# Cross-attention with a softmax over the queries: exp kept in PSUM, VectorE's row group of y kept in a PSUM bank, both halves of v made from PSUM

## The reference

```python
q = jnp.einsum('bte,ef->btf', emb, Wq) + bq
k = jnp.einsum('bml,le->bme', latent, Wk) + bk
v = jnp.einsum('bml,le->bme', latent, Wv) + bv
w = jnp.einsum('bte,bme->btm', q, k) * scale          # scale = 1/sqrt(512)
w = jax.nn.softmax(w, axis=1)                         # over t
pred = jnp.einsum('btm,bme->bte', w, v)
x = pred + emb
mu = jnp.mean(x, axis=-1, keepdims=True)
var = jnp.var(x, axis=-1, keepdims=True)
return (x - mu) * jax.lax.rsqrt(var + EPS) * gamma + beta
```

## Time and profile before

| | us |
|---|---|
| runs | 232.30, 232.39, 232.49 (median 232.39) |
| the profiled execution | 232.25 |
| its span, first to last instruction | 230.4 |
| PE, busy (share of the span) | 194.9 (85%) |
| DVE | 180.1 (78%) |
| POOL | 168.5 (73%) |
| ACT | 161.5 (70%) |
| mean granted TensorE clock | 0.953 of full speed |

### The profile page before, as it was taken

The page is one execution under the profiler, slowest core; times in us unless marked ns, Lnnn a source line. Parts: engine busy times, 40 slices in busy tenths (PEclk is TensorE's granted clock), DMA queues, the critical chain, the costliest instruction groups (busy, mean ns, idle before and its releaser), DMA issues.

```text
span 230.4 us, 4152 instructions
## 1 busy us (share of the span) xinstructions
PE 194.9 (85%) x1168; PEld 119.2 (52%) x1168; DVE 180.1 (78%) x453; ACT 161.5 (70%) x343; POOL 168.5 (73%) x163
## 2 busy tenths in 40 slices
PE   4888699978999999899999998999999999876100
PEld 4745567464657464646474656565656564342000
DVE  0498854898979697869796978697969798698993
ACT  2534768369787979696969695969696969764510
POOL 1000003038999999999999999999999999994790
PEclk9999999999999999999999999999999999996555
DMA  5999991002464646454646464646464540404045
GB/s 153 300 234 336 372 354 44 3 1 54 195 223 189 216 188 226 179 186 189 215 188 216 175 235 171 213 176 226 159 226 182 182 183 0 186 0 182 0 182 182
DMA packets 11914, 41.04 MB, mean 178 GB/s; under 512 B 1022, under 2 KB 5886, under 8 KB 8062
## 3 DMA queue, kind: packets, MB, share of 16 engines
q1 hardware_dynamic: 11614, 40.37, 49.5%
q10 hardware_dynamic: 288, 0.52, 0.9%
HBM read 24.12 MB, written 16.78 MB: 177 GB/s over the span
## 4 chain that ended last, share of the span: by engine, by line
POOL 43%; issue 15%; DVE 13%; PE 11%; DMA 7%; ACT 5%; SPq 1%; DVEq 1%; POOLq 1%; ACTq 0%
POOL obuf L969 17%; POOL obuf L963 13%; DMA obuf<-in_ctx 7%; POOL rstd L996 5%; PE s_ps L426 4%; POOL v_part L956 3%; ACT obuf L618 3%; POOL square_mean L982 2%; DVE obuf L824 2%; DVE prob_part L810 2%; DVE xbuf L842 2%; PE g_ps L396 2%; PE pv_ps L418 1%; DVE key_junk L702 1%; ACT xT L555 1%
## 5 line engine op out<-in xcount | busy, mean ns | idle before, releaser
L426 PE MATMUL s_ps<-xT,gT 128*120 128x512 f32 x128 | 57.9, 593 | 0.9 <-ACT xT L555 0.9
L963 POOL TENSOR_TENSOR obuf<-obuf,gamma_all 128x512 f32<-128x512 f32 x44 | 56.1, 1301 | 2.0 <-ACT obuf L618 2.0
L969 POOL TENSOR_TENSOR obuf<-obuf,beta_all 128x1536 f32<-128x1536 f32 (+1 forms) x16 | 51.8, 3236 | 1.2
L618 ACT ACTIVATE obuf<-xbuf,shift,rstd 128x512 f32<-128x512 f32 x44 | 32.8, 804 | 14.5 <-POOL shift L1001 14.5
L418 PE MATMUL pv_ps<-v_part,prob_part 120*128 120x512 f16 x135 | 36.1, 380 | 5.9 <-issue 2.1
L426 PEld LDWEIGHTS s_ps<-xT,gT 128*120 128x120 f32 x128 | 23.2, 183 | 27.2 <-issue 20.7
L404 PEld LDWEIGHTS xT_ps<-ident,xbuf 128*128 128x128 f32 x256 | 29.6, 140 | 12.7 <-issue 8.2
L404 PE MATMUL xT_ps<-ident,xbuf 128*128 128x128 f32 x256 | 33.4, 274 | 2.1 <-ACT xT L555 1.6
L555 ACT ACTIVATE xT<-xT_ps 128x512 f32<-128x512 f32 x64 | 33.9, 580 | 1.0 <-PE xT_ps L404 1.0
L956 POOL TENSOR_TENSOR v_part<-v_scaled,v_part 120x512 f16<-120x512 f32 x16 | 24.9, 1557 | 11.6 <-ACT v_part L588 11.3
L842 DVE SCALAR_TENSOR_TENSOR xbuf<-pv_ps,back_y,xbuf 128x512 f32<-128x512 f32 x45 | 32.4, 744 | 0.1
(11 more groups left out here) (114 smaller groups left out, 281.3 us busy)
## 6 DMA issues: line engine op xcount, KB each, us to landing
xbuf<-in_x SPq DMA_DIRECT2D x16, 1024.0 KB, 4.8
out<-obuf SPq DMA_DIRECT2D x14, 1024.0 KB, 4.2
out<-obuf SPq DMA_DIRECT2D x8, 256.0 KB, 2.5
ctx_nat<-in_ctx SPq DMA_DIRECT2D x16, 120.0 KB, 4.3
obuf<-in_ctx SPq DMA_DIRECT2D x2, 960.0 KB, 14.6
wq_nat<-in_L_xattn_Wq SPq DMA_DIRECT2D x2, 512.0 KB, 8.7
wk_nat<-in_L_xattn_Wk SPq DMA_DIRECT2D x1, 512.0 KB, 5.7
wv<-in_L_xattn_Wv SPq DMA_DIRECT2D x1, 512.0 KB, 12.9
```

Source lines behind the costliest of these rows:

```text
L426: mm = pe.matmul(s_ps[0:M, :], gT[:, k % 2, e, :], xT[:, e, :], start=(e == 0), stop=(e == EC - 1))
L618: act.activation(obuf[:, k % 2, j, :], xbuf[:, kn, j, :], ACT.Identity, bias=shift[:, j:j + 1], scale=rstd[:, k % 2, j:j + 1]).then_inc(no ...
L963: pool.tensor_tensor(obuf[:, k % 2, j, :], obuf[:, k % 2, j, :], gamma_all[:], ALU.mult)\
L969: done = pool.tensor_tensor(obuf[:, k % 2, 0:share, :], obuf[:, k % 2, 0:share, :], beta_all[:].unsqueeze(1).broadcast_to([P, share, E]), ...
```

## The change

Five things are changed together.

1. Exp is written back into the bank of the scores. ScalarE's high half and VectorE's low half of the probabilities read it there. Batch 14 alone still uses the SBUF tile `probs`.
2. The row groups of y that VectorE normalises itself (the fourth; from batch 14 on the second to fourth) stay in a PSUM bank: residual, statistics or square, centre and rescale read and write there, and only rescale writes `obuf`. The fourth product goes to `ctx_ps` for that; the context of batches 3 and up is turned into an `xT_ps` bank instead, and the two `xT_ps` banks change their roles from batch to batch.
3. bv is added by TensorE: one more matmul in front of the six of v, of a tile of constants with the scaled bv in two halves, 64 rows each.
4. Both halves of v come straight out of `v_ps`: the high one by ScalarE with its scale, the low one by VectorE. The fp32 copy and GpSimd's part are gone; `v_part` has four buffers instead of two.
5. ScalarE makes the high half of v after exp instead of at a slot's start. Before the loop, a reciprocal, a split of bv and a memset are added, and the scaling of bv in fp32 is gone.

The core of the diff:

```diff
+        def held(s, j):
+            return j >= 1 if is_slot(s, B - 1) or is_slot(s, B) else j == RJ - 1
+        def probs_of(b):
+            return probs[:] if is_slot(b, B - 2) else s_ps[0:M, :]
+        def y_of(s, kb, j):
+            return y_banks(s)[j] if held(s, j) else xbuf[:, kb, j, :]
-        y_ps = [bank_[:] for bank_ in (pv_ps[0], pv_ps[1], v_ps, pv_ps[0])]
+        y_ps = [bank_[:] for bank_ in (pv_ps[0], pv_ps[1], v_ps, ctx_ps)]
...
             def turn_ctx(b, k, r):
-                if is_in(b, 1, B):
-                    pe.wait_ge(ctx_low, b)
+                if isinstance(b, int) and b < FIRST_CTX:
+                    if b > 0:
+                        pe.wait_ge(ctx_low, b)
+                else:
+                    pe.wait_ge(xT_copied, EC * (b - 2) + EC - 1)
...
             def context_v(b, k):
                 pe.wait_ge(ctx_low, b + 1)
                 if is_in(b, 1, B):
-                    pe.wait_ge(v_copied, b)
+                    pe.wait_ge(v_low, b)
...
+                pe.matmul(v_ps[0:M, :], bias_ones[:], bv_part[:], start=True, stop=False)
...
             def product(b, k, j):
...
-                    pe.wait_ge(v_copied, b + 3)
-                if j == 3 and is_in(b, 0, B - 1):
-                    pe.wait_ge(y_done, RJ * b + 1)
+                    pe.wait_ge(v_low, b + 3)
+                if j == 3 and is_slot(b, 0):
+                    pe.wait_ge(ctx_low, FIRST_CTX)
+                elif j == 3 and is_slot(b, B - 1):
+                    pe.wait_ge(y_done, RJ * (B - 2) + 1)
+                elif j == 3:
+                    pe.wait_ge(dve_out, b)
...
-            pe.wait_ge(high_split, 3)
-            pe.wait_ge(low_split, 3)
+            pe.wait_ge(bias_set, 1)
+            pe.wait_ge(low_split, 4)
             context_v(0, 0)
...
-                act.activation(v_part[:, parity, HIGH], v_scaled[:, parity], ACT.Copy).then_inc(v_high, 1)
+                    act.wait_ge(v_done, b + 1)
+                    act.activation(v_part[:, k, HIGH], v_ps[0:M, :], ACT.Copy, scale=onto_v[0:M, :])\
+                        .then_inc(v_high, 1)
...
-                    act.activation(probs[:], s_ps[0:M, :], ACT.Exp, bias=s_bias[:], scale=SCALE,
+                    act.activation(probs_of(b), s_ps[0:M, :], ACT.Exp, bias=s_bias[:], scale=SCALE,
                                    accum_out=s_sum[:]).then_inc(probs_done, 1)
...
+            scales(dve.reciprocal(bound_rec[:], bound[:, 0:1]))
             low_part(qk_part[:, LOW, 0, :], g_ps[:], scale[:, 1:2], qk_part[:, HIGH, 0, :], 1)
...
+            low_part(bv_part[BIAS_ROWS:, :], bv_all[BIAS_ROWS:, :], bv_by[BIAS_ROWS:, :], bv_part[BIAS_ROWS:, :], 4)
...
-                dve.scalar_tensor_tensor(v_scaled[:, k % 2], v_ps[0:M, :], onto_v[0:M, :], bv_scaled[0:M, :],
-                                         ALU.mult, ALU.add).then_inc(v_copied, 1)
+            def v_to_low(b, k):
+                dve.wait_ge(v_high, b + 1)
+                dve.scalar_tensor_tensor(v_part[:, k, LOW], v_ps[0:M, :], onto_v[0:M, :], v_part[:, k, HIGH],
+                                         ALU.mult, ALU.subtract).then_inc(v_low, 1)
...
                     else:
                         dve.wait_ge(sums_negated, B if s == B else B + RJ)
-                    dve.wait_ge(obuf_free[k % 2], obuf_fills(k, r))
-                    dve.scalar_tensor_tensor(obuf[:, k % 2, j, :], xbuf[:, kn, j, :], by, gamma_all[:], op, ALU.mult)\
-                        .then_inc(dve_gamma, 1)
+                        dve.wait_ge(squares_done, SQUARE_J * (B - 2) + RJ * (s - B + 1))
+                    y = y_of(s - 1, kn, j)
+                    dve.scalar_tensor_tensor(y, y, by, gamma_all[:], op, ALU.mult).then_inc(dve_gamma, 1)
...
-                if is_in(s, 0, B):
-                    pool.wait_ge(v_high, s + 1)
-                    pool.tensor_tensor(v_part[:, k % 2, LOW], v_scaled[:, k % 2], v_part[:, k % 2, HIGH],
-                                       ALU.subtract).then_inc(v_low, 1)
```

More of the change, by code:

```diff
@@ L51 @@
 TAIL = 2
+FIRST_CTX = 3
 SQUARE_J = 2
@@ L60 @@
 BACK_FIELD = 14
-LEAST_BOUND = 2.0 ** -100
+LEAST_BOUND = 2.0 ** -60
+BIAS_ROWS = 64
+BIAS_SCALE = 2.0 ** 15
 CTX_PARTS = 4
@@ L161, in cross_attention, with ctxT_view @@
         pv_ps = [bank(f"pv_ps{i}", [P, 512]) for i in range(2)]
-        y_ps = [bank_[:] for bank_ in (pv_ps[0], pv_ps[1], v_ps, pv_ps[0])]
-        last_y_ps = [*(bank_[:].rearrange("p j q -> p (j q)") for bank_ in xT_ps), ctx_ps[:], g_ps[:]]
-        ctxT_v = ctx_ps[:, 0:LC * M].rearrange("p (c m) -> p c m", m=M)
+        y_ps = [bank_[:] for bank_ in (pv_ps[0], pv_ps[1], v_ps, ctx_ps)]
+        flat_xT_ps = [bank_[:].rearrange("p j q -> p (j q)") for bank_ in xT_ps]
+        last_y_ps = [*flat_xT_ps, g_ps[:], pv_ps[0][:]]
+        def ctxT_view(b, k):
+            of = ctx_ps[:] if isinstance(b, int) and b < FIRST_CTX else flat_xT_ps[k % 2]
+            return of[:, 0:LC * M].rearrange("p (c m) -> p c m", m=M)
         g_v = g_ps[:, 0:EC * M].rearrange("p (c m) -> p c m", m=M)
@@ L385, in context_v @@
                     mm = pe.matmul(v_ps[0:M, :], ctxT[:, k % 2, of_ctx, c, :], wv_part[:, of_w, c, :],
-                                   start=(n == 0), stop=(n == len(steps) - 1))
+                                   start=False, stop=(n == len(steps) - 1))
                 mm.then_inc(v_done, 1)
@@ L497, in slot @@
                     pe.wait_ge(prob_high, s)
-                    product(s - 1, k + 1, 0)
-                    product(s - 1, k + 1, 1)
-                    product(s - 1, k + 1, 2)
+                    product(s - 1, kb, 0)
+                    product(s - 1, kb, 1)
+                    product(s - 1, kb, 2)
                 if is_in(s, 0, B - 2):
@@ L503, in slot @@
                 if last:
-                    product(s - 1, k + 1, 3)
+                    product(s - 1, kb, 3)
                 if main and not is_slot(s, B - 1):
@@ L573, in _ @@
             copy_g(0, 0)
-            copy_xT(0, 2)
-            copy_xT(0, 3)
+            copy_xT(0, 0, 2)
+            copy_xT(0, 0, 3)
             ctx_to_high(1, 1)
@@ L624, in slot @@
                         ctx_to_high(2, 2)
+                    if is_in(s, 2, B - 1):
+                        v_to_high(s + 1, (k + 1) % RING)
                     probs_to_high(s - 1)
-                if is_slot(s, 1):
-                    v_to_high(0, 0)
                 if is_slot(s, B - 1):
-                    copy_xT(s, 2)
-                    copy_xT(s, 3)
+                    copy_xT(s, k, 2)
+                    copy_xT(s, k, 3)
                 if is_in(s, 2, B) or is_slot(s, B + 1):
                     normalise()
-                if main and not is_slot(s, B - 1):
-                    copy_xT(s, 2)
-                    copy_xT(s, 3)
                 if is_slot(s, 1):
                     v_to_high(1, 1)
+                if main and not is_slot(s, B - 1):
+                    copy_xT(s, k, 2)
+                    copy_xT(s, k, 3)
+                if is_slot(s, 1):
+                    v_to_high(2, 2)
                 if is_in(s, 1, B - 2):
@@ L761, in _ @@
             dve.wait_ge(max_bounds, 2)
-            dve.tensor_copy(bound[:, 2:3], max_bound[:, WV:WV + 1])
             dve.wait_ge(dve_bounds, 4)
+            dve.scalar_tensor_tensor(bound[:, 2:3], bound_rec[:], bv_bound[:], max_bound[:, WV:WV + 1],
+                                     ALU.mult, ALU.max)
             scales(dve.scalar_tensor_tensor(bound[:, 3:4], bound[:, 0:1], max_bound[:, WV:WV + 1], bv_bound[:],
```

90 lines of the change are left out of this document (49 added, 41 removed).

## The result

| | before | after |
|---|---|---|
| runs | 232.30, 232.39, 232.49, 233.31 | 222.76, 222.42, 221.15, 222.34 |
| median | 232.44 | 222.38 |
| span of the profiled execution | 230.4 | 220.9 |

The ratio is 0.9553, 95% interval 0.951 to 0.9597. The forecast was 221.6.

The account below looks back on a forecast made before the run. GpSimd was taken to bound the kernel (43% of the chain of waits). Loop gives 4.3, head takes 2.2, tail gives 8.6: slot 15 at 192.2 plus 27.5 makes span 219.7, time 221.6; range 218.2 to 226.3, including rival 1.

Parts of the forecast that it names:

- TensorE becomes the bound, 10.9 a slot: Loop: TensorE bounds in place of GpSimd; 10.53, plus 0.21 for the bv matmul, plus a stall taken as 0.15.
- Rival 1: Loop gives nothing: the context's turn waits 0.4 to 0.5 a slot for ScalarE; 11.25 a slot, 225.5; chance 0.16.
- GpSimd is freed: Loop: GpSimd loses the low half of v (1.67) and 0.45 of square_mean; its cycle falls from 11.28 to 10.1.
- VectorE and GpSimd are separated by PSUM operands: Loop and tail: with one operand in PSUM, VectorE and GpSimd no longer stop each other; last low half 3.84 becomes 0.75.
- rival 2: One PSUM and one SBUF operand still stops for GpSimd; 7.2 of the tail stays, slot grows 0.05: 229.3; chance 0.06.
- Writing PSUM costs nothing: Exp, fourth residual and centre: no change in time from writing PSUM; bounds a 0.05 gain to 0.74 more each.
- rival 3: Writing PSUM is slow in exp, fourth residual and centre: 0.3 more each gives 224, 0.74 gives 236; chance 0.08.
- The head, 2.2 with bounds 1.2 to 2.8: Before the loop: added splits and bv matmuls make slot 2 start 1.95 later, slot 3 at 61.75 instead of 59.54.
- The tail, 27.5: From slot 15's start to the end: 36.1 falls by 8.6 to 27.5.
- the first two terms: Tail: slot 15's centre falls from 2.50 to 0.75, gaining 1.1; the last probabilities' low half, 3.84 to 0.75, gains 3.1.
- the third: Tail: the products after TensorE's gap no longer run at the low clock; three intervals gain 1.4.
- the fourth: Tail: last two batches' centres and rescales take 8.2 instead of 12.1; 0.9 held back for GpSimd's last group, gaining 3.0.

Follow-up runs that it names:

- the second pair of traces: The kernel after and the kernel before, both unaltered, run again for a second trace each: 221.47 (ratio 0.9525) and 231.43.
- the second trace of before: The kernel before, unaltered, run again for a second trace: 231.43 for the one run.
- the second trace: The kernel after, unaltered, run again for a second trace of its head: 221.47, ratio 0.9525.

## Why the prediction was right, and where it was not

- **TensorE becomes the bound, 10.9 a slot.** 10.85. The matmul for bv costs its 0.21 (the run without it), the wait of the turn of the context 0.10 (the run with the copy moved), where 0.15 was taken. Rival 1 is out: the mechanism is there, at a quarter of its size.
- **GpSimd is freed.** Right, but half of the reason was wrong. The prediction took the low half of v off GpSimd's path at its full 1.67. With the PSUM parts in place it takes 1.16, so 0.5 of it was stalling, and these 1.16 lie in a wait for ScalarE's normalise that is there anyway (1.68 without them, 0.49 with them), so that the kernel with v still on GpSimd is as fast. What frees the loop is above all that VectorE no longer holds two SBUF operands; without that the rest of the change takes 0.16 off a slot. The forecast could not fail by this, since both parts came together; as a guide to what to keep it would have misled.
- **VectorE and GpSimd are separated by PSUM operands.** Shown by the last low half and by the kernel without the PSUM parts; rival 2 is out.
- **Writing PSUM costs nothing.** Centre and fourth residual 752, exp 670 where it was 689: rival 3 is out. The 0.065 more for a PSUM source that the prediction took from the Trainium skill (VectorE: DVE Perf Modes, section on the TRN2 errata) isn't seen either: VectorE's low half takes 743 out of PSUM and 752 out of SBUF, its statistics 698 and 686, a fifth of that.
- **The head, 2.2 with bounds 1.2 to 2.8.** This step failed: slot 3 came 5.3 later. The terms themselves were nearly right; from landing to slot 3 a trace with the full clock takes 42.0 against 39.3, so 2.65. The other 2.6 are the landing (1.5) and the low clock (1.1). The prediction took one trace's head as fixed, and had no term for either. Some 0.7 of the landing goes with the change, as its transfer takes longer; the issue and the clock belong to the execution, and by the second pair of traces slot 3 comes 3.5 later.
- **The tail, 27.5.** 26.2. Up to the last products it gains 4.35 (the first two terms: 4.2), then 1.47 (the third: 1.4), then 4.05 (the fourth: 3.0). The third term belongs to the execution and not to the kernel: in the second trace of before the clock stays full there and 3.78 lie between the last products and the first centre behind them, 3.89 after the change. The 0.9 held back in the fourth for GpSimd's last group wasn't needed: it ended 0.47 behind VectorE, at 217.77, and 3.6 lie behind VectorE's last rescale as they did before.

So the head's miss of 3.1 was set off by the tail (1.3) and the loop (0.6), which leaves 1.2 in the span; the median lies 0.4 below the traced execution, and the time came out within 0.8. Part of that closeness is luck: the clock fell in the tail of the trace before (1.6 more there) and in the head of the trace after (1.1 more), and the two nearly cancel.

## What to carry to other kernels

When a change has several parts that relieve the same engine, price each with the others already in place: a stalled instruction's length is partly the stall, and a freed engine may only wait elsewhere. A VectorE instruction with two SBUF operands beside a busy GpSimd is worth moving one operand to PSUM for, above all where a long GpSimd instruction meets the critical path once. And where the profile before is one execution, give the head and the tail of the program a term for how transfers and clock vary.

## What the runs showed of the hardware that was not expected

- The wait between VectorE and GpSimd goes both ways, within one slot: VectorE's low half 1.38 behind GpSimd's 1.16, then GpSimd's three multiplies 4.19 in place of 3.74.
- ScalarE gets a little faster with its source in PSUM: the high half of the probabilities 681 ns, 0.72 us out of SBUF.
- A fall of the granted clock in the head cost 1.6 at the first scores, but only 1.1 at slot 2, since with the full clock TensorE waits 0.38 for VectorE's splits in front of v of batch 0: the last of them ends at 34.78 in the second trace, and v begins at 34.88.
- Waits of TensorE of the same length, 3.19 and 3.18, at the same place of the kernel before were followed by a granted clock of 0.50 in one trace and of 1.00 in the other.
